# One pass of normalisation over two PSUM banks, three of four low halves on GpSimd, one column for each expert sum, and new chunk tables in a cross-attention and expert kernel

## What is computed

```
x = x + cross_attention(layernorm(x), ctx, ctx, Wq, bq, Wk, bk, Wv, bv, Wo, bo)   # 16 heads of 32, 77 keys
h = layernorm(x)
chosen = argmax(h @ gate_w.T)             # one of 8 experts for each token
x = x + h @ expert_w[chosen].T            # each expert is a 512 x 512 matrix
```

## Time and profile before

| | |
|---|---|
| median of 3 runs | 1016.04 us (1012.83 to 1017.89) |
| profiled execution, its own time | 1020.97 us |
| span of the profiled execution | 1019.20 us |
| PE busy | 922.2 us, 90% of the span |
| DVE busy | 793.0 us, 78% |
| ACT busy | 558.6 us, 55% |
| POOL busy | 540.9 us, 53% |
| mean granted clock of TensorE | 0.95 |

### The profile page before, as it was taken

One profiled execution on the slowest core, in us unless ns is written; L12 is line 12 of the kernel. 1 busy time (PEld: TensorE's weight loads), 2 busy tenths in 40 slices (PEclk: granted clock), 3 DMA queues, 4 the chain that ended last, 5 costly groups with the idle time before them and its releaser, 6 DMA issues. The chain is left out here.

```text
span 1019.2 us, 27541 instructions
## 1 busy us (share of the span) xinstructions
PE 922.2 (90%) x8838; PEld 549.9 (54%) x8839; DVE 793.0 (78%) x1828; ACT 558.6 (55%) x928; POOL 540.9 (53%) x553
## 2 busy tenths in 40 slices
PE   5759699999989999989999999999783999999996
PEld 3234555655556555655566555656662555555553
DVE  7746888998979889888899998978876556565663
ACT  4355476776847768658686686774833112121210
POOL 3022445456454654645556555464443577777774
PEclk9877799999989999989999999999886999999998
DMA  9211134244342441533414343224624355555550
GB/s 319 76 41 33 33 95 136 53 135 109 86 135 59 136 136 45 141 82 114 140 43 134 86 119 116 61 75 139 228 108 153 110 166 175 160 169 170 167 179 26
DMA packets 82792, 119.52 MB, mean 117 GB/s; under 512 B 22001, under 2 KB 47141, under 8 KB 82671
## 3 DMA queue, kind: packets, MB, share of 16 engines
q1 hardware_dynamic: 69935, 81.87, 29.9%
q0 software_dynamic: 11664, 36.05, 9.3%
q10 hardware_dynamic: 1072, 0.02, 0.1%
HBM read 55.24 MB, written 38.13 MB: 92 GB/s over the span
## 5 line engine op out<-in xcount | busy, mean ns | idle before, releaser
L527 POOL TENSOR_TENSOR p_lo<-pf,p_hi 77x512 f16<-77x512 f32 x128 | 151.7, 1191 | 222.3 <-ACT p_hi L1085 221.9
L1084 ACT ACTIVATE pf<-scoresT,exp_scale 77x512 f32<-77x512 f32 x256 | 175.2, 684 | 85.6 <-PE scoresT L818 78.3
L1567 PE MATMUL mo<-e_w,x2T_hi 128*128 x576 | 184.4, 382 | 0.7 <-DVE x2T_lo L1604 0.7
L1085 ACT ACTIVATE p_hi<-scoresT,exp_scale 77x512 f16<-77x512 f32 x256 | 175.6, 686 | 0.0
L1587 ACT ACTIVATE x2T_hi<-mt 128x512 f16<-128x512 f32 x72 | 43.1, 598 | 183.5 <-PE mt L1556 183.5
L1614 DVE SCALAR_TENSOR_TENSOR res<-mo,inv,row 128x512 f32<-128x512 f32 x72 | 54.0, 750 | 91.1 <-PE mo L1567 88.9
L527 DVE TENSOR_TENSOR p_lo<-pf,p_hi 77x512 f16<-77x512 f32 x128 | 109.5, 871 | 11.0 <-ACT p_hi L1085 9.5
L1172 DVE TENSOR_REDUCE negmax<-work 128x4 f32<-128x308 f32 x256 | 112.4, 467 | 0.4 <-PE work L870 0.3
L1567 PE MATMUL mo<-e_w,x2T_lo 128*128 x288 | 109.9, 382 | 0.0
L1538 POOL DMA_INDIRECT out<-res,row x72 | 71.5, 994 | 65.0 <-DVE xn L1599 56.8
L790 PE MATMUL work<-xnT_hi,wq_hi 128*128 128x512 f16 x256 | 99.1, 387 | 4.3 <-DVE xnT_lo L1150 2.5
(11 more groups left out here) (256 smaller groups left out, 2205.1 us busy)
## 6 DMA issues: line engine op xcount, KB each, us to landing
row<-rows_by_expert SPq DMA_DIRECT2D x72, 257.5 KB
q_st<-q_hi SPq DMA_DIRECT2D x256, 64.0 KB, 2.0
xt<-in_x SPq DMA_DIRECT2D x15, 1024.0 KB, 8.6
q_st<-q_lo SPq DMA_DIRECT2D x128, 64.0 KB, 2.0
ebuf<-in_L_ffn_expert_w SPq DMA_DIRECT2D x14, 512.0 KB, 7.4
er<-in_L_ffn_expert_w SPq DMA_DIRECT2D x7, 1024.0 KB, 15.1
out<-res,row POOLq DMA_INDIRECT x72, 2.7
xt<-in_x SPq DMA_DIRECT2D x4, 256.0 KB, 6.2
```

Of the source, the lines that this page charges most:

```text
L527: return tt.tensor_tensor(pp[1][0:LK, g % 2, j, :], pf[:, j, :], pp[0][0:LK, g % 2, j, :], ALU.subtract)
L1084: nc.scalar.activation(pf[:, j, :], sbank[n % SB][0:LK, :], ACT.Exp, scale=exp_scale[0:LK, :])
L1085: nc.scalar.activation(pp[0][0:LK, g % 2, j, :], sbank[n % SB][0:LK, :], ACT.Exp, scale=exp_scale[0:LK, :]).then_inc(sem("exp_done"), 1)
L1567: ins = nc.tensor.matmul(obank2[u % 2][:, :], x2T[ia][:, u % 2, k, :], w, start=k == 0 and n == 0, stop=k == KT - 1 and n == 2)
```

## The change

- `P_DVE` is 1: head 0 of a group stays on DVE, heads 1, 2 and 3 are POOL's.
- The two banks of the values become one tensor of two banks, 128 x 4 x 256. `values` fills all four token tiles and signals once; `normalise` runs once for a group, over both banks, with one reciprocal of 128 x 16 and one product of 128 x 512. PE begins a group's values only when the whole group before is normalised.
- `sum_piece` writes each sum into a column of its own; `piece_max` and its 16 steps go, and one reduction over the 16 columns in iteration 13 takes their place. What waited for `e_maxed` (the load of the next piece, the next sum) waits for `e_summed`.
- All chunk tables are new. In the table of PE the step `NM` comes first, all eight transposes `T` and `C` stand together behind it, and then the scores.

```
-P_DVE = 2
+P_DVE = 1
...
 STEPS = order("""
-    T0 T1 NM C0 T2 C1 T3 O0 C2 S00 S01 Q0 S02 S03 O1 S10 M00 C3 S11 M01 Q1 S12 PV0 S13 M02 GC M03 M10 S20 S21 M11 M12
-    O2 M13 S22 S23 Q2 R S30 S31 PV1 M20 Q3 S32 M21 S33 M22 PV2 M23 O3 M30 GX PV3 M31 M32 M33
+    NM T0 T1 C0 C1 T2 T3 C2 C3 S00 S01 O0 S02 S03 Q0 S10 O1 M00 M01 S11 S12 Q1 S13 M02 PV0 S20 GC S21 M03 M10 O2 S22
+    S23 M11 Q2 R M12 PV1 S30 S31 M13 M20 Q3 M21 S32 O3 S33 M22 M23 M30 PV2 M31 GX M32 PV3 M33
 VECTOR = order("""
...
-    M12 V00 V01 O2 M13 B2 Q2 R EM0 V10 V11 M20 SL P30 Q3 V20 M21 M22 M23 V21 P31 O3 M30 B3 GX VE V30 M31 M32 M33 V31
+    V1 M12 M13 P30 SL M20 Q3 B2 M21 O3 M22 M23 M30 V2 M31 B3 GX VE M32 M33 V3
...
 GPSIMD = order("""
-    A0 A1 A2 P02 P03 A3 P12 P13 F P22 P23 P32 P33 G D
+    A0 P01 P02 P03 A1 P11 A2 P12 P13 P21 P22 F P23 P31 P32 P33 G A3 D
...
-    den = sa("den", [P, 2, 2, HG])
+    den = sa("den", [P, TPC, HG])
...
-        obank = [st.enter_context(nc.psum_tensor(f"pv{c}", [P, 512], F32)) for c in range(2)]
+        obank = st.enter_context(nc.psum_tensor("pv", [P, TPC, 256], F32))
...
-                wait_alone(sp, "e_maxed", sum_number(i, 0) - 1)
+                wait_alone(sp, "e_summed", sum_number(i, 0) - 1)
...
-                for h in range(2):
-
-                    pe.wait_ge(sem("normalised"), 2 * G + h + 1)
-                    for t in (2 * h, 2 * h + 1):
-                        for j in range(HG):
...
+                pe.wait_ge(sem("normalised"), G + 1)
+                for t in range(TPC):
+                    for j in range(HG):
...
-                nc.scalar.activation(ebuf[par][:], src, ACT.Abs, accum_out=e_sum[:, par:par + 1])\
+                nc.scalar.activation(ebuf[par][:], src, ACT.Abs, accum_out=e_sum[:, bass.ds(sum_number(i, k), 1)])\
...
-            def normalise(i, g, h):
...
+            def normalise(i, g):
+                dve.wait_ge(sem("values_ready"), KT * i.n + g + 1 + 2)
+                o = obank[:, :, 0:HG * VC].rearrange("p t (j k) -> p t j k", j=HG)
+                do(nc.vector.reciprocal(den[:], o[:, :, :, DK]))
+                nc.vector.tensor_tensor(cc[:, :, g * P:(g + 1) * P].rearrange("p t (j k) -> p t j k", j=HG),
+                                        o[:, :, :, 0:DK], den[:].unsqueeze(3).to_broadcast([P, TPC, HG, DK]), ALU.mult)\
...
+                if i.is_(NCHUNK - 3):
+
+                    dve.wait_ge(sem("e_summed"), 2 * E)
+                    nc.vector.tensor_reduce(mx_e[:], e_sum[:], X, ALU.max).then_inc(sem("e_maxed"), 1)
...
-            def piece_max(i, k):
-                par = sum_par(i, k)
-                dve.wait_ge(sem("e_summed"), sum_number(i, k) + 1)
-                nc.vector.tensor_tensor(mx_e[:], mx_e[:], e_sum[:, par:par + 1], ALU.max).then_inc(sem("e_maxed"), 1)
```

More of the change, by code:

```diff
@@ L100 @@
 VECTOR_FIRST = order("""
-    T0 T1 AR T2 T3 AS WQ0 WQ1 WQ2 WQ3 KL Q0 OM0 OM1 OM2 OM3 BM L0 Q1 M00 M01 M02 M03 BR L1 Q2 M10 M11 M12 M13 BS GS L2 L3
-    Q3 M20 M21 M22 M23 LE GX DV0 M30 M31 M32 M33 DV1 DV2 DV3 CV
+    T0 T1 AR T2 T3 AS WQ0 WQ1 WQ2 WQ3 KL Q0 OM0 OM1 OM2 OM3 BM L0 Q1 M00 M01 M02 M03 BR L1 Q2 M10 M11 M12 M13 BS GS L2
+    L3 Q3 M20 M21 M22 M23 LE GX DV0 M30 M31 M32 M33 DV1 DV2 DV3 CV
 """)
@@ L114 @@
 VECTOR_ZERO = order("""
-    NM T0 T1 P00 P01 T2 T3 WO0 Q0 WO1 M00 M01 DW0 DW1 L0 L1 P10 P11 Q1 M02 WO2 DW2 DW3 M03 L2 M10 EM0 M11 L3 M12 LE
-    P20 P21 V00 V01 DT M13 EM1 WO3 Q2 DG V10 V11 M20 P30 Q3 EM2 V20 M21 DB M22 M23 V21 P31 DK GB M30 GX V30 M31 M32 EM3
-    M33 V31
+    NM T0 T1 P00 T2 T3 WO0 Q0 WO1 M00 M01 DW0 DW1 L0 L1 P10 Q1 M02 WO2 DW2 DW3 M03 L2 M10 M11 L3 M12 LE P20 V0 DT M13
+    WO3 Q2 DG V1 M20 P30 Q3 M21 DB M22 M23 V2 DK GB M30 GX M31 M32 M33 V3
 """)
@@ L123 @@
 GPSIMD_ZERO = order("""
-    P02 P03 P12 P13 F P22 P23 P32 P33 A0 A1 A2 A3
+    P01 P02 P03 P11 P12 P13 F P21 P22 P23 P31 P32 P33 A0 A1 A2 A3
 """)
@@ L130 @@
 VECTOR_LAST = order("""
-    NM C0 C1 C2 C3 O0 B0 P00 P01 O1 B1 O2 B2 P10 GC H O3 B3 VE P11 E00 E01 P20 R SL V00 V01 E02 E03 P21 E10 E11
-    V10 V11 P30 E12 E13 P31 E20 E21 V20 V21 E22 E23 V30 V31
+    NM C0 C1 C2 C3 O0 B0 P00 O1 B1 O2 B2 P10 GC H O3 B3 VE E00 E01 P20 R SL V0 E02 E03 E10 E11 V1 P30 E12 E13 E20 E21
+    V2 E22 E23 V3
 """)
@@ L267, in build @@
     mx_2 = sb("mx_2", [1, 1], BF16)
-    e_sum = sb("e_sum", [P, 2])
+    e_sum = sb("e_sum", [P, 2 * E])
     pows = sb("pows", [P, 2, TPC])
@@ L462, in build @@
         scale_bank = sbank[1]
-        v_bank = [obank[1], obank[0], sbank[0], sbank[1]]
+        o_half = [obank[:, 2 * n:2 * n + 2, :].rearrange("p t d -> p (t d)") for n in range(2)]
+        v_bank = [o_half[1], o_half[0], sbank[0], sbank[1]]
         v_order = [0, 1, 2, 3]
@@ L759, in prologue @@
                 for k in range(KT):
-                    ins = nc.tensor.transpose(obank[0][:, k * E:(k + 1) * E], g8[:, k * P:(k + 1) * P], ident[0:E, 0:E])
+                    ins = nc.tensor.transpose(o_half[0][:, k * E:(k + 1) * E], g8[:, k * P:(k + 1) * P], ident[0:E, 0:E])
                 ins.then_inc(sem("g_filled"), 1)
@@ L826, in values @@
                 pe.wait_ge(sem("p_lo_pool"), (HG - P_DVE) * (G + 1) + HG)
-                for h in range(2):
-                    pe.wait_ge(sem("normalised"), 2 * G + h + 1)
-                    for t in (2 * h, 2 * h + 1):
-                        for j in range(HG):
[L832 to L838, removed]
+                pe.wait_ge(sem("normalised"), G + 1)
+                for t in range(TPC):
+                    for j in range(HG):
+                        for n, (ip, iv) in enumerate(HL):
+                            ins = nc.tensor.matmul(obank[:, t, j * VC:(j + 1) * VC],
+                                                   pp[ip][:, g % 2, j, t * P:(t + 1) * P], v_now[iv][:, g * HG + j, :],
+                                                   start=n == 0, stop=n == 2)
+                ins.then_inc(sem("values_ready"), 1)
             def banked(i, kind, *at):
@@ L1092, in _ @@
         def _(dve):
-            own = OwnCount(21)
+            own = OwnCount(17)
             def mark(ins):
@@ L1105, in _ @@
             dve.nop().then_inc(sem("stack_built"), 1)
-            dve.nop().then_inc(sem("normalised"), 2)
-            dve.nop().then_inc(sem("values_ready"), 4)
+            dve.nop().then_inc(sem("normalised"), 1)
+            dve.nop().then_inc(sem("values_ready"), 2)
             dve.nop().then_inc(sem("pay_stats"), 1)
@@ L1316, in prologue @@
                 early(nc.vector.memset(mb[:], 0.0))
-                early(nc.vector.memset(mx_e[:], 0.0))
                 clear(v_all[1])
@@ L1488, in iteration @@
                         own_parts[kind](i, *at)
-                        if (kind, *at) == ("V", KT - 1, 1) and i.slot == CPB - 1 and not i.is_(NCHUNK - 1):
+                        if (kind, *at) == ("V", KT - 1) and i.slot == CPB - 1 and not i.is_(NCHUNK - 1):
                             copy_v(i.plus(1).batch)
```

25 lines of the change are left out of this document (9 added, 16 removed).

## The result

The changed kernel takes **1033.58 us** in the median of 4 runs (1025.68 to 1035.69); the kernel before took 1016.96 in the runs made beside it and before. The ratio is 1.0165, with a 95% interval of 1.013 to 1.02: slower by 17 us, where 1009.0 was forecast and the range ended at 1021.

A forecast was written before the change was run, and what follows sets the result against it. PE was taken as the bound, busy 922 of 1019 us, with DVE close behind in the 14 chunks. Chunk 0 -4, the 14 chunks -3, last chunk 0: -7 from 1016.04 gives 1009.0 us, range 993 to 1021.

The forecast's parts named there:

- Chunk 0: First chunk: low half no longer held, but `GB` held by five POOL additions; `nmT` about 120.5 against 125.58, 4 us gained.
- Last chunk: Last chunk of the stage: PE's order stays, ACT's exponentials and expert halves pace it; change 0.
- The new wait of `NM`: Border of two chunks, `NM` directly behind `M33`: PE waits 1.2 us for the last negated maxima.
- The nine transposed steps: Border, `NM` and eight transposed tiles: the ninth step starts about 4.7 us after `NM` instead of 4.0.
- No difference: Border, from `NM` to first product: a stall of 0.7 us against 0.8 today, so no change.
- rival A: Clock falls at the new borders, up to 1.7 us each; 1033 us if at all 14; chance 18%.
- Rival B: `nmT` lands late, or POOL holds DVE elsewhere; 0.4 us more each, +5.6, 1015 us; chance 17%.
- Today the border costs 11.2/14 = 0.8: Border in the kernel before: PE's 11.2 us of waits for negated maxima, spread over 14 chunks, 0.8 us each.
- +0.4 a chunk: Border: the wait of `NM` becomes 1.2 us where today it costs 0.8, a loss of 0.4 us a chunk.
- 17 us: PE's waits for negated maxima, `q_lo` and `nmT` in 14 chunks: the most a lighter DVE can give.
- None of that is on PE's path except through the waits above: Inside the chunks: DVE loses 5 us a chunk, which reaches PE only through its listed waits.
- a gain of 0.6 us a chunk: Inside a chunk: `q_lo` 0.25, late `nmT` 0.15, held low halves and `mx_e` perhaps 0.25; together -0.6.

The follow-up runs named there:

- e1: Changed kernel with `S33` moved ahead of `O3` in PE's table: 1025.69 us, ratio 1.0108 to the kernel before.
- e8: Changed kernel with the transfer of `nmT` issued by ACT instead of SP, `S33` left late: 1025.05 us, ratio 1.009 to the kernel before.
- e3: Changed kernel with `S33` ahead of `O3` and four products of 128 x 512 ahead of `NM`: 1015.82 us, ratio 1.0024 to the kernel before.
- e9: Kernel before the change, plus column sums and one-pass normalisation, old tables, two low halves on DVE: 1006.01 us, ratio 0.9904.
- e13: Kernel before the change, plus the column sums alone: 1008.21 us, ratio 0.9916.
- e4: Changed kernel with the chunk tables of the kernel before, the rest of the change kept: 1019.21 us, ratio 1.0052 to the kernel before.

## Why the prediction was wrong

**Right.** *Chunk 0*: `GB` was held 6.33 us by the row of five, `nmT` came at 120.90 (forecast 120.5). *Last chunk*: no change. *Durations*: one pass takes 0.25 + 0.69 us, forecast 0.2 + 0.69. *The new wait of `NM`*: 0.7 to 1.1 us, 1.0 in the mean, forecast 1.2. *The nine transposed steps*: 4.7 us from `NM` to the first product, once clock and queue are clear.

**The step that failed first** is "No difference", for the stretch from `NM` to `S00`. It took 6.6 us in the mean, not 4.7. Two things were missing: the time of the transfer and the clock. The transfer of `nmT` was taken to start when `nmT` was done. I had not followed `S33`, which moved past `O3`, to the twelve transfers that wait for it on SP ahead of `nmT`: 8 us by e1 and e8. And the clock falls at 8 of the 12 borders where the loop does not jump back. That is rival A, which I gave 18%, on the evidence of a border at 0.51 right behind such a wait. By e3 against e1 it is worth up to 10 us, 5.9 of them in the 14 chunks. Rival B named the right transfer at 0.4 us each; the waits were up to 3.2.

**A term of the same border was mis-sized.** "Today the border costs 11.2/14 = 0.8" divides a sum in which 6.5 us are the two waits where the loop jumps back, which the change leaves alone. An ordinary border cost 0.4. With the forecast's own 1.2 us for `NM`, the 12 ordinary borders would have cost about 10 us more, not the 5.6 of "+0.4 a chunk"; measured are 7.1. It also means that of the "17 us" of waits a lighter DVE had some 10 to earn: the two waits at the jumps stayed in e9 and e13 (6.9 and 6.6 us), where DVE is lighter.

**The second step that failed** is "None of that is on PE's path except through the waits above", as far as the low halves go. The forecast put a gain of 0.6 us a chunk on `q_lo`, the late `nmT` and the holding together, and no cost at all on the low halves that POOL takes. In the old tables the sums alone gain 8 us, about what that term had for everything, and the low halves lose 13. The evidence was in the rows: `mx_e` at 901 ns, and 12 waits for `q_lo`, one a chunk. I did not ask which DVE work stands just ahead of `q_lo`. I also counted 2.75 us a chunk off DVE for the low halves, while holding, which I had used for chunk 0, took it back: with the old tables DVE's busy time rose by 4 us instead of falling by 39 (14 x 2.75).

**The sum as the runs have it,** from one kernel to the next. Column sums -7.9, one pass -1 to -2, low halves +13, tables +14 (1033.6 against 1019.2), of which the queue 8 and, with the products, the clock 10, which is more than the 14, since e3 is 3 us faster than e4. Together +18, where 17 to 18 were measured. These steps lead through the old tables, so the sum closes by its making and does not show what each part costs inside the changed kernel. The +13 of the low halves is net of chunk 0, where they gain 4.6 us (`nmT` at 119.3 instead of 123.9). Rival A's 1033 is near the result, but by another sum, so it is no support for it.

## What to carry to other kernels

When a step moves, follow everything that waits for it, the DMA queues too: a small transfer stands behind a dozen that wait for a late score. Before dividing a sum of waits by the number of chunks, look at its largest members. Moving work to GpSimd was no relief for VectorE where both read SBUF at the same moment: add up the holding, one operation at a time, ahead of the instruction whose bank TensorE needs next. Tiny two-input operations cost VectorE what is left of the GpSimd instruction beside them (0.90 us here, 0.15 alone), so one reduction at the end earned 8 us, where the 16 operations that it replaces would have taken 2.4 unhindered.

## What was unexpected of the hardware

```profile
L1452 DVE SCALAR_TENSOR_TENSOR gx<-gx,inv,gate_c x1: 8115/8115/8115, 111.4 to 111.4; 128x32 f32<-128x32 f32 x1
```

- At 8 of the 12 ordinary borders of the changed kernel, with waits of PE of 1 us at seven of them, the clock lies for 3.4 or 6.8 us at the level of 1.2 GHz, and twice it falls before the wait. Filling the wait with transposes or with four products removed 34 us of the 57.8.
- SP needs 0.63 us for each `q_st` transfer that it issues, so twelve of them close its queue for 7.5 us.
